# Attention's mask: products on TensorE or a write by ScalarE

## What is computed

```
x = x + 0.5 * ffn(layernorm(x))
x = x + attn(layernorm(x))
x = x + 0.5 * ffn(layernorm(x))
```

```
qh = qb @ wq + bq;  kh = kb @ wk + bk;  vh = vb @ wv + bv
scores = (qh / 8) . kh            # 128 x 128 per head and block
scores = where(causal, scores, -1e9)
ctx = softmax(scores) . vh
out = (ctx @ wo + bo) @ proj_w + proj_b
```

## Time and profile before

| | |
|---|---|
| median of 3 runs | 743.78 us (742.42 to 744.44) |
| span of the profiled execution, first to last instruction | 739.8 us |
| TensorE busy in the span | 681.5 us, 92% |
| VectorE | 530.7 us, 72% |
| ScalarE | 490.4 us, 66% |
| GpSimd | 337.7 us, 46% |
| mean granted TensorE clock | 0.977 of full speed |

### The profile page before, as it was taken

One profiled execution on the slowest core, in us unless ns is written; L12 is line 12 of the kernel. 1 busy time (PEld: TensorE's weight loads), 2 busy tenths in 40 slices (PEclk: granted clock), 3 DMA queues, 4 the chain that ended last, 5 costly groups with the idle time before them and its releaser, 6 DMA issues. The chain is left out here.

```text
span 739.8 us, 19381 instructions
## 1 busy us (share of the span) xinstructions
PE 681.5 (92%) x5481; PEld 598.2 (81%) x5481; DVE 530.7 (72%) x1834; ACT 490.4 (66%) x1733; POOL 337.7 (46%) x361
## 2 busy tenths in 40 slices
PE   3999799999999899999999999999879999999854
PEld 3986699999995678888888888888568999999743
DVE  6588566666665777787878787877868777777553
ACT  5776566666664477887877777777645666666643
POOL 4200644444433654446666666362646444444500
PEclk9999899999999999999999999999979999999978
DMA  9940344544442211111111111010324643434299
GB/s 306 307 143 1 111 144 147 146 129 129 129 121 79 88 36 40 34 29 59 58 60 58 59 58 59 30 59 2 94 94 142 176 132 122 127 123 126 72 328 352
DMA packets 57865, 83.42 MB, mean 113 GB/s; under 512 B 9520, under 2 KB 43827, under 8 KB 57780
## 3 DMA queue, kind: packets, MB, share of 16 engines
q1 hardware_dynamic: 44772, 47.63, 20.7%
q0 software_dynamic: 13008, 34.69, 14.8%
HBM read 45.77 MB, written 37.44 MB: 112 GB/s over the span
## 5 line engine op out<-in xcount | busy, mean ns | idle before, releaser
L1693 PE MATMUL CC<-w_hi,turned_parts 128*128 x568 | 173.9, 348 | 1.1 <-DVE turned_parts L1258 1.1
L692 POOL DMA_INDIRECT shared<-h_rows,tok_i x71 | 70.0, 986 | 115.1 <-DVE tok_i L1165 42.1
L1693 PEld LDWEIGHTS CC<-w_hi,turned_parts 128*128 128x128 f32 x568 | 104.9, 192 | 1.7 <-issue 1.6
L709 POOL DMA_INDIRECT y_rows<-shared,y_dest x71 | 69.9, 985 | 71.5 <-DVE y_dest L1271 56.3
L725 POOL TENSOR_TENSOR pr<-pr,prec 128x1024 f32<-128x1024 f32 x31 | 58.7, 1894 | 83.9 <-DVE prec L1466 83.9
L771 ACT ACTIVATE shared<-CC 128x176 f32<-128x176 f32 x142 | 45.1, 317 | 74.4 <-PE CC L1693 74.4
L1693 PE MATMUL CC<-w_lo,turned_parts 128*128 x284 | 92.4, 325 | 0.0
L862 ACT ACTIVATE pr<-SS,nmax 128x128 f32<-128x128 f32 x256 | 90.3, 404 | 1.4 <-DVE nmax L1436 1.4
L1252 DVE TENSOR_TENSOR shared<-shared,CC 128x176 f32<-128x176 f32 x142 | 47.9, 338 | 47.4 <-ACT shared L771 44.1
L742 POOL DMA_INDIRECT h_regions<-h_store,dest x64 | 62.7, 979 | 41.9 <-DVE dest L1358 24.6
L733 POOL DMA_INDIRECT yg<-y_rows,slot_i x64 | 62.4, 975 | 34.0 <-DMA y_rows<-shared 15.5
(11 more groups left out here) (349 smaller groups left out, 2005.2 us busy)
## 6 DMA issues: line engine op xcount, KB each, us to landing
yg<-h_regions SPq DMA_DIRECT2D x71, 129.0 KB
y_rows<-shared SPq DMA_DIRECT2D x71, 128.0 KB, 1.7
w_lo<-y_rows SPq DMA_DIRECT2D x9, 512.0 KB, 8.1
x_sb<-in_x_dram SPq DMA_DIRECT2D x8, 512.0 KB, 8.1
out_dram<-x_sb SPq DMA_DIRECT2D x16, 256.0 KB, 6.0
w_hi<-y_rows SPq DMA_DIRECT2D x7, 512.0 KB, 11.5
w_lo<-in_gupT_dram SPq DMA_DIRECT2D x2, 1408.0 KB, 12.5
h_regions<-pad_rows SPq DMA_DIRECT2D x15, 129.0 KB, 2.7
```

Source lines behind the costliest of these rows:

```text
L692: pool.indirect_dma_start(out=rows[:, s % RING, 0:D], out_offset=None, in_=h_dram[:, :], in_offset=bass.IndirectOffsetOnAxis(ap=tok_i[:, s ...
L709: pool.indirect_dma_start(out=y_dram[0:TOPK * TOKENS, :], out_offset=bass.IndirectOffsetOnAxis(ap=y_dest[:, s:s + 1], axis=0), in_=y_sb[:, ...
L1693: i = pe.matmul(CC[:, 512 * (u % 2):512 * (u % 2) + GU], rows_part[:, u % 2, c * P:(c + 1) * P], weights, start=(n == 1), stop=(n == 3 * DC))
```

## The change

ScalarE gets an instruction, `write_mask`, which copies `mask_bf` eight times side by side into SS, over both banks. It stands in each turn i behind the exponentials, the copy into G and ha, and ahead of hr, where there are tiles i and i+1; it waits for the exponentials of turn i and counts `exp` up once more. TensorE's two mask products are gone from turns 1 to 31; TensorE waits for the mask write instead and then adds the scores to what stands in SS. In turn 0 TensorE makes two mask products with `keep_clock`. The reciprocal's wait is renumbered.

```diff
@@ ScalarE
+                def write_mask():
+                    a.activation(SS[:, :].rearrange("p (h s) -> p h s", s=P),
+                                 mask_bf[:, :].unsqueeze(1).to_broadcast([P, NH, P]), ACT.Copy).then_inc(t["exp"], 1)
...
                         a.activation(ha[:, q, :], x_tile(b), ACT.Identity, bias=shift[:, 0:1], scale=arstd[:, 0:1]
                                      ).then_inc(t["normed"], 1)
+                    if there(i) and there(i + 1):
+                        a.wait_ge(t["exp"], 2 * i + 1)
+                        write_mask()
                     if there(i - 3):
                         b, q = i - 3, (u - 3) % GROUP
@@ VectorE
                     if there(i):
-                        v.wait_ge(t["exp"], i + 1)
+                        v.wait_ge(t["exp"], 2 * i + 1)
                         v.reciprocal(prec[:, u % 2, :], psums[:, u % 2, :]).then_inc(t["rec"], 1)
@@ TensorE
                     if there(i):
-                        after(pe, t["exp"], i)
-                        for half in range(2):
-                            pe.matmul(SS[:, 512 * half:512 * (half + 1)], ident_bf[:, :], mask_4,
-                                      start=True, stop=False, skip_group_check=True)
+                        if i == 0:
+                            for half in range(2):
+                                keep_clock(SS[:, 512 * half:512 * (half + 1)], 1)
+                        else:
+                            pe.wait_ge(t["exp"], 2 * i)
                         pe.wait_ge(t["qkh_sb"], i + 1)
```

## The result

| | before | changed |
|---|---|---|
| median | 743.14 us (742.42 to 744.44, 4 runs) | 737.86 us (737.03 to 738.3, 4 runs) |
| ratio | | 0.9933 [0.9919, 0.9948] |
| second measurement | 742.30 us | 738.81 us, ratio 0.9953 [0.9939, 0.9967] |
| span of the profiled execution | 739.8 us | 736.6 us (second: 737.1) |
| TensorE, VectorE, ScalarE, GpSimd busy | 681.5, 530.7, 490.4, 337.7 us | 670.4, 529.5, 519.2, 339.4 us |

The kernel became 0.5 to 0.7% faster: 5.3 us in the first measurement, 3.5 us in the second. The forecast was 3.5 us.

A forecast was written before the change was run, and what follows sets the result against it. TensorE was taken to bound attention, VectorE one turn in four. Turns 0 to 10 +0.4, 10 to 26 -3.7, 26 to 31 -0.2: -3.5 us, span 736.3, median 740.3 us; own range 738.5 to 742.3, wider 737.4 to 744.0.

The forecast's parts named there:

- The offsets: From S(i), the start of turn i's scores: ScalarE's L853 at S + 2.22, mask write at S + 7.07 us.
- From the write's start to the scores: ScalarE's mask write plus hand-over to TensorE's scores: 1.24 to 1.36 us from the rows, taken as 1.35.
- the path at 8.42 us: Attention turns: scores wait for the mask write, so S(i+1) is at least S(i) + 7.07 + 1.35 us.
- the forecast loss of 0.40: Turns 0 to 10: S(0) to S(10) takes 84.88 us where it was 84.48, +0.40 us.
- turns 0 to 8 longer than before: Sign to look for in early attention turns: most go to 8.42 us, set by the mask write.
- The saving in q/k turns: Turns with 18 q/k convolution products: without mask products TensorE takes 0.53 us less, 8.50 us.
- The picking pair: Two turns around VectorE's top-2 picking: evict starts 9.52 us after the one before, 17.67 us for both turns.
- Turn 27: Near attention's end, TensorE waits for GpSimd's normalisation, queued behind four row sends: 1.03 us of the gain lost.
- The last turn: Turn 30 to 31: the mask write takes L881's place, scores at 522.49 against 522.31, +0.18 us.
- The write as the path of every turn: Rival, slower: write start to scores takes 1.71 us or more, about +2 us, at 1.83 about +4; chance 0.13.
- Cancelling out: Rival: write start to scores near 1.6 us, or v-turn waits pushing GpSimd or VectorE: 743.9 us; chance 0.22.
- The hidden write: Rival: TensorE starts within 0.7 us of the write, VectorE sets the pace: about -9 us, 735 us; chance 0.05.

The follow-up runs named there:

- the earlier place: Changed kernel with the mask write ahead of ha, behind G's copy: ratios to the kernel before 0.9909, 0.9929 and 0.9942 (737.37 us) in three runs.
- the loss behind the exponentials: Changed kernel with the mask write directly behind the exponentials, ahead of the copy into G: 793.44 us against 790.07 of before, ratio 1.002.

## Why the prediction was right, and where its terms were off

The forecast was 740.3 us; the runs gave 737.86 and 738.81, and the sign and the mechanism are those of the prediction. From the kernel of before measured beside them (743.14 and 742.30), the change is -5.3 and -3.5 us where -3.5 was forecast. That the second agrees to the digit is luck: attention gained 5.0 and 5.2 us in the two profiles, 1.5 or more above the forecast's sum, and the second lost 2.1 us behind S(31). 737.86 lies below the forecast's own range (from 738.5), within the wider one (from 737.4).

*The offsets.* The write starts at S + 7.08 (forecast 7.07) and L857 still at S + 2.22. Moving the write 0.49 us later made a q/k turn 8.71 us and lost the gain, doubling it made 25 of 31 turns 9.28 or 9.29 us. Shown.

*From the write's start to the scores: forecast 1.35 us, measured 1.15.* This is the term that was off, by size. The record was right: about 1.1 forecast, 1.09 measured. The hand-over was not: 0.26 us from the end of G's copy to the ranks' product, where the mask's is 0.06. Of the 0.22 to the ranks' weight load, 0.11 hung on the order of TensorE's waits. It put the path at 8.42 us instead of 8.23 in all v turns and early turns. S(0) to S(10): five turns 0.19 or 0.20 shorter than forecast and one (7 to 8) too, S(1) 0.22 earlier (7.97 for 8.19), and 0.17 given back in the q/k turn and the picking pair. That is 84.88 - 83.67 = 1.21 us, and turns the forecast loss of 0.40 into a gain of 0.81. The sign "turns 0 to 8 longer than before" did not come: S(0) to S(8) is 65.91 us against 66.29. The estimate from the Trainium skill ("ScalarE: Activation LUTs", What ACT_TABLE_LOAD costs) came nearer here: its 1.04 us for the instruction is 0.05 below the record, and the path of 8.31 us worked out with it is 0.08 above the measured one. Duration and hand-over erred against each other in it.

*The saving in q/k turns: forecast 0.53 us, measured 0.43 to 0.47 (0.34 once, from S(10)).* These turns go to 8.57 to 8.60 us (8.69 once), not to 8.50. The timeline of TensorE at the end of such a turn, before and then changed:

```profile
380.30 0.28 PE L1774 MATMUL B<-turned_parts,conv_qk_hi 128*128 128x256 f32 x1
380.43 0.60 PE L1790 MATMUL SS<-mask_bf,ident_bf 128*128 128x512 bf16 x2
380.96 1.16 PE L1795 MATMUL SS<-shared 64*128 64x128 f32 x16
```

```profile
380.16 0.28 PE L1781 MATMUL B<-turned_parts,conv_qk_hi 128*128 128x256 f32 x1
380.38 0.83 PE L1803 MATMUL SS<-shared 64*128 64x128 f32 x10
```

From the last convolution product to the scores it is 0.66 us before and 0.22 after. The mask product stood 0.13 behind the convolution product; the scores stand 0.22 behind it. I had subtracted the distance from mask product to scores as if the scores would then take the mask product's place, but they start 0.09 later than it did. What makes the 0.09 isn't shown; in both traces the first load of the scores' weights starts with their first product (380.96 and 380.38).

*The picking pair: forecast 17.67 us, measured 17.71 to 17.80,* the group 34.63 and 34.54 in the first two (forecast 34.63). The rule VectorE's evict to evict held, 9.51 us, but the scores start 1.32 us behind the evict's start and not 1.26, since they follow its end by 0.15. The group's v turn was 0.19 shorter and its first turn 0.04 to 0.15 longer than forecast. In the kernel of before the prediction puts TensorE's wait ahead of the ranks (L1886) to VectorE's picking as well; there it is ScalarE's copy into G, which ends 0.22 us before the ranks' weight load in every picking turn of the groups. In the changed kernel that copy ends 0.43 to 0.50 us before it, so it no longer sets this place.

*Turn 27: forecast 1.03 us lost to GpSimd.* TensorE of the changed kernel:

```profile
484.02 1.16 PE L1803 MATMUL SS<-shared 64*128 64x128 f32 x16
487.12 1.09 PE L1811 MATMUL CC<-ident,pr 128*128 128x128 f32 x8 [1.94 <-POOL pr L725]
...
494.25 1.16 PE L1803 MATMUL SS<-shared 64*128 64x128 f32 x16 [0.28 <-ACT SS L824]
```

It waits 1.94 us where it waited 0.86: 1.08 us given back. S(27) to S(28) is 10.23 us against 9.25.

*The last turn.* Forecast +0.18; S(30) to S(31) is 7.58 against 7.48, with VectorE's evict and the mask write ending at the same time.

*The rivals.* The write as the path of every turn (x, from the write's start to the scores, 1.71 us or more) is out: x is 1.15, and the doubled write shows what it would have been. Cancelling out needed x near 1.6. The hidden write was out of reach in this place. In the earlier place it is hidden behind VectorE's evict, and the group is 34.45 us and not the 34.05 of that rival, since the evict sets v turns at 7.94 and the q/k turn behind them is 8.78. The rows show the change as written: TensorE's products are gone and its scores wait for L824. No row shows the accumulate bits. The Trainium skill ("PSUM — Partial Sum Buffer", The four PSUM rules) has a product without start add to ScalarE's data where the bits are set, and here turn 0's products with start have set them.

*What stays open:* how much of the loss behind the exponentials the delayed copy into G explains; how long v turns are without any mask; which wait makes TensorE 0.15 us slower between L1819 and L1758 in the earlier write; why the mask's hand-over is 0.06 us where three others are 0.11 or 0.12; what lost 2.1 us behind S(31) in the second profile.

## What to carry to other kernels

Where a step moves from the engine that bounds a stage to one with idle time, what counts is the offset at which it can start, plus its duration, plus the hand-over; the mean busy share of the second engine says nothing of that. Read a hand-over from a place where the wait in question is the last of its engine's waits, since in this kernel another wait behind it added 0.11 us that looked like the first's. And ahead of a step that is meant to go beside others, work out which engine's release is next (here VectorE's evict, 0.29 us on): it is the most that moving the step can bring. And what an instruction costs on the path is not the distance to the next one: see how far behind its predecessor the next would start in its place.

## What the runs showed of the hardware that I had not expected

- A ScalarE copy of 128x1024 from a broadcast bf16 tile in SBUF over two PSUM banks takes 1.09 us (1.06 in turn 0, and 1.03 where it follows the exponentials or another such copy). G's f32 copy of 352 columns takes 0.54, and 672 more at 0.84 ns would make 1.10: nothing was lost to the broadcast, the type or the bank's edge.
- From its end to TensorE's dependent product it is 0.05 to 0.06 us, to f32 and bf16 products alike. From the copy into G, from hT and from VectorE's evict to TensorE's load it is 0.11, 0.11 and 0.12.
- TensorE's ranks loaded their weights 0.11 us later where other semaphore waits stood behind the one that came last (0.22 against 0.11 us from the copy's end).
